# Normalised rows turned by VectorE and moved through DRAM: a one-core hybrid block

## The reference, cut to what matters

```
x = x + scan_layer(layernorm(x))      # projections, gated scan, product
x = x + ffn(layernorm(x))             # gelu(x @ W1t + b1) @ W2t + b2, hidden width 1024
x = x + attention(layernorm(x))       # 16 heads of 64, second-order linear attention
x = x + ffn(layernorm(x))             # the same weights again
```

## Time and profile before

| what | value |
|---|---|
| median of three executions | 1029.08 us (1025.98 to 1030.72) |
| the profiled execution, its own time | 1030.74 us |
| its span, first to last instruction | 1029.0 us |
| mean granted TensorE clock | 0.998 of full speed |
| TensorE busy | 1005.3 us |
| VectorE busy | 617.2 us |
| ScalarE busy | 491.0 us |
| first layer, to 97.3 us | TensorE busy 91.81 us |
| first feed-forward, 97.3 to about 227 us | tasks 16.06 us apart |
| attention, about 227 to 895 us | chunks some 20 us apart |
| last feed-forward alone, from 895.4 us | DMA share 0.11 |

### The profile page before, as it was taken

One profiled execution on the slowest core, in us unless ns is written; L12 is line 12 of the kernel. 1 busy time (PEld: TensorE's weight loads), 2 busy tenths in 40 slices (PEclk: granted clock), 3 DMA queues, 4 the chain that ended last, 5 costly groups with the idle time before them and its releaser, 6 DMA issues.

```text
span 1029.0 us, 41963 instructions
## 1 busy us (share of the span) xinstructions
PE 1005.3 (98%) x19166; PEld 909.2 (88%) x19166; DVE 617.2 (60%) x1252; ACT 491.0 (48%) x925; POOL 111.4 (11%) x130
## 2 busy tenths in 40 slices
PE   8999999999999999999999999999999999999998
PEld 7788798999998998899999999988899888889887
DVE  7888877763445545555465465553564457767773
ACT  5676766643343433333443344333443344456663
POOL 2461331220000000000000000000000000113130
PEclk9999999999999999999999999999999999999999
DMA  9422000023324233242242333332333333200101
GB/s 314 154 59 82 1 2 1 1 83 115 115 85 131 90 95 126 69 143 85 96 136 90 101 124 101 111 101 69 126 106 106 104 126 94 97 22 21 42 31 52
DMA packets 60735, 92.75 MB, mean 90 GB/s; under 512 B 7056, under 2 KB 50448, under 8 KB 59536
## 3 DMA queue, kind: packets, MB, share of 16 engines
q1 hardware_dynamic: 60288, 90.07, 26.6%
q10 hardware_dynamic: 272, 0.00, 0.0%
HBM read 48.63 MB, written 41.42 MB: 88 GB/s over the span
## 4 chain that ended last, share of the span: by engine, by line
PE 95%; ACT 2%; issue 1%; DVE 1%; POOL 0%; POOLq 0%; ACTq 0%; DVEq 0%
PE bank L223 7%; PE bank L224 6%; PE bank L1185 6%; PE bank L225 6%; PE bank L1211 6%; PE bank L1196 5%; PE bank L1245 4%; PE bank L1233 3%; PE bank L1175 3%; PE bank L1222 3%; PE bank L805 3%; PE bank L807 3%; PE bank L1246 3%; PE bank L1247 3%; PE bank L1261 3%; PE bank L1177 3%
## 5 line engine op out<-in xcount | busy, mean ns | idle before, releaser
L1471 ACT COPY qt<-bank 128x512 f32<-128x512 f32 x64 | 37.6, 587 | 157.0 <-PE bank L225 157.0
L1607 DVE STREAM_TRANSPOSE k<-kt 128x512 f32<-128x512 f32 x64 | 43.4, 697 | 106.6 <-ACT kt L1466 55.6
L1466 ACT COPY kt<-bank 128x512 f32<-128x512 f32 x64 | 37.5, 587 | 114.5 <-PE bank L225 114.5
L1628 DVE TENSOR_TENSOR state_s<-bank,state_s 128x256 f32<-128x256 f32 x124 | 46.8, 420 | 74.5 <-ACT ut L1484 72.5
L223 PE MATMUL bank<-ln_xhi,wk_hi 128*128 128x256 f32 x256 | 75.9, 296 | 0.0
L223 PE MATMUL bank<-ln_xhi,wq_hi 128*128 128x256 f32 x256 | 75.4, 294 | 0.0
L1245 PE MATMUL bank<-wo_hi,ot_hi 128*128 128x256 f32 x256 | 75.0, 293 | 0.0
L1518 ACT ACTIVATE D_hidden<-bank,b_sb 128x512 f32<-128x512 f32 x64 | 44.1, 690 | 59.6 <-PE bank L1262 59.6
L224 PE MATMUL bank<-ln_xlo,wk_hi 128*128 128x256 f32 x256 | 72.5, 283 | 0.0
L224 PE MATMUL bank<-ln_xlo,wq_hi 128*128 128x256 f32 x256 | 72.3, 283 | 0.0
L225 PE MATMUL bank<-ln_xhi,wk_lo 128*128 128x256 f32 x256 | 72.3, 282 | 0.0
(11 more groups left out here) (161 smaller groups left out, 2904.9 us busy)
## 6 DMA issues: line engine op xcount, KB each, us to landing
k_rows_scratch<-k SPq DMA_DIRECT2D x32, 512.0 KB, 2.7
k<-k_rows_scratch SPq DMA_DIRECT2D x128, 128.0 KB, 2.9
u_rows_scratch<-sc_and_k SPq DMA_DIRECT2D x31, 512.0 KB, 3.4
landed<-u_rows_scratch SPq DMA_DIRECT2D x124, 128.0 KB, 3.0
out_dram<-xres SPq DMA_DIRECT2D x16, 256.0 KB, 2.1
xres<-in_L_attn_a_x_dram SPq DMA_DIRECT2D x7, 512.0 KB, 10.5
w_nat<-in_L_ffn_W_dram SPq DMA_DIRECT2D x2, 1024.0 KB, 9.8
raw<-in_L_attn_b_W_q_dram SPq DMA_DIRECT2D x1, 1024.0 KB, 12.9
```

## The change

In both feed-forwards and in the attention the normalised rows are no longer turned by TensorE. VectorE turns 32x32 blocks of `ln.xn` into a tile (two instructions of 128x512), SyncE writes the tile to a DRAM scratch with one DMA, waits for it, and reads it back into `ln.xn` with four DMAs. ScalarE and VectorE then take `xhi` and `xlo` from SBUF instead of PSUM. The turns in the first layer stay with TensorE, and so does that of the first block of the first feed-forward. Where the rows go to the attention, the copies and subtractions are in quarters: four instructions of 128x256 instead of two of 128x512.

The order changes with it. In a feed-forward task the rows are normalised at f = 2 of the same task in which their statistics were taken at f = 1, and turned at f = 3, ahead of `xlo` at f = 4 (in task 1 of the last feed-forward they are normalised at f = 5 and turned at f = 6, and `xlo` moves from f = 6 to behind that). In the attention the statistics, the normalising and the turn come one chunk earlier (chunks 3 and 4 instead of 4 and 5, and so on), and `xhi` and `xlo` stay in chunk 5. The block of task (0,0) has its statistics in chunk 27 and is normalised and turned in chunk 28, that of (0,1) in chunks 28 and 29, and the next block of batch 0 is normalised and turned in chunk 31.

```diff
+            def dve_turn(self, dve, slot, tile, count):
+                if count:
+                    dve.wait_ge(self.rows_saved, 16 * count)
+                src = self.xn[:, slot, :, :].rearrange("p c d -> p (c d)").rearrange("p (n g f) -> p g n f", g=4, f=32)
+                for n in range(2):
+                    nc.vector.transpose(tile[:, :, 4 * n:4 * n + 4, :], src[:, :, 4 * n:4 * n + 4, :]).then_inc(self.rows_turned, 1)
+
+            def sp_move(self, sp, slot, tile, count):
+                if count:
+                    sp.wait_ge(self.rows_landed, 64 * count)
+                sp.wait_ge(self.rows_turned, 2 * (count + 1))
+                sp.dma_start(rows_dram["x"], tile.rearrange("p g n f -> p g (n f)")).then_inc(self.rows_saved, 16)
+                sp.wait_ge(self.rows_saved, 16 * (count + 1))
+                for g in range(4):
+                    sp.dma_start(self.xn[g * 32:(g + 1) * 32, slot, :, :],
+                                 rows_dram["x"].rearrange("(r p) g c -> g p r c", r=4)[g]).then_inc(self.rows_landed, 16)
...
+            def act_high_rows(self, act, b, count):
+                act.wait_ge(self.rows_landed, 64 * (count + 1))
                 for k in range(DC):
+                    nc.scalar.copy(self.xhi[:, b, k, :].rearrange("p (c r i) -> p c r i", c=CH, r=4),
+                                   self.landed(b, k)).then_inc(self.high_done[b], 1)
...
@@ first feed-forward, TensorE: the turns go @@
-                            if target and f == 3:
-                                prepare(target[0], target[2])
...
@@ first feed-forward, VectorE @@
-                        if target:
-                            tb, block_of_rows, n = target
-                            dve.wait_ge(ln.rstd_done[tb], START + n + 1)
-                            ln.dve_normalise(dve, tb, block_of_rows, n, ln_rstd)
...
+                            if f == 2:
+                                dve.wait_ge(ln.rstd_done[b], START + n0 + i + 2)
+                                ln.dve_normalise(dve, b, 0 if last else i + 1, n0 + i + 1, ln_rstd)
+                            if f == 3:
+                                dve.wait_ge(ln.normalised[b], START + (n0 + i + 2) * CH)
+                                ln.dve_turn(dve, b, turned, moves(b, i))
                             if target and f == 4:
-                                ln.dve_low(dve, tb, n, XB)
+                                ln.dve_low_rows(dve, target[0], target[2])
...
@@ attention, SyncE: the move goes behind keys and u; the last one ahead of the reload of W2 @@
+                    if norm_of(j):
+                        ln.sp_move(sp, norm_of(j) % 2, turned_x, chunk_moves(norm_of(j) - 2))
+                    if block_of(j) is not None:
+                        ln.sp_move(sp, block_of(j), turned_x, moves(block_of(j), 0))
...
+                ln.sp_move(sp, 0, k32, moves(0, 1))
                 sp.wait_ge(v_ready, 2 * CHUNKS)
                 sp.dma_start(wv_hi[:, :, :].rearrange("p a b -> p (a b)").bitcast(FP32), w2t_dram).then_inc(w2_loaded, 16)
...
@@ attention, VectorE @@
+                    elif block_of(j + 1) is not None:
+                        if block_of(j + 1) == 0:
                             dve.wait_ge(x_added, 8)
+                        ln.dve_statistics(dve, block_of(j + 1), 0, nd)
                     if norm_of(j):
+                        chunk_normalise(norm_of(j) - 2)
+                    elif block_of(j) is not None:
+                        normalise_for(block_of(j), 0)
+                        turn_for(block_of(j), 0, turned_x)
...
@@ ScalarE: the first gelu of the last feed-forward (its tile shares memory with the turned rows) @@
+                    if n == 0:
+                        act.wait_ge(ln.rows_saved, 16 * (moves(1, 0) + 1))
...
@@ last feed-forward, VectorE @@
+                        if f == started + 2 and i + 1 < NBLK:
+                            normalise_for(b, i + 1)
+                        if f == started + 3 and i + 1 < NBLK:
+                            turn_for(b, i + 1, k32)
+                        if target and f == high_at(t):
+                            ln.dve_low_rows(dve, target[0], nd + target[1])
```

More of the change, by code:

```diff
@@ L753, in sync @@
                 sp.dma_start(w2t_dram, w2t.rearrange("p a b -> p (a b)").bitcast(FP32)).then_inc(w_saved, 16)
+                for i in range(NBLK):
+                    for b in range(B):
+                        ln.sp_move(sp, b, turned, moves(b, i))
                 sp.wait_ge(out_ready[0], START + 2 * NBLK)
@@ L810, in down @@
                         last.then_inc(out_ready[b], 1)
[L812 to L817, removed]
                 def iteration(i, first, last):
                     for b in range(B):
[L821 removed]
+                        behind = former(b, i, first)
                         for f in range(FC):
@@ L833, in tail @@
                 def tail():
[L834 to L837, removed]
+                    for part in range(FC):
+                        down(1, NBLK - 1, part)
                 steps(iteration, tail)
@@ L868, in tail @@
                     for b in range(B):
+                        act.wait_ge(ln.rows_landed, 64 * (moves(b, NBLK - 1) + 1))
                         for k in range(DC):
[L870 to L873, removed]
+                            for s in range(2):
+                                last = nc.scalar.copy(of_turns(ln.xhi, s, k, b), landed_of_turns(b, k, s))
+                            last.then_inc(ln.high_done[b], 1)
                 steps(iteration, tail)
@@ L924, in tail @@
                             dve.wait_ge(ln.high_done[b], START + (n0 + NBLK) * DC + k + 1)
[L925 to L928, removed]
+                            for s in range(2):
+                                last = nc.vector.tensor_tensor(of_turns(ln.xlo, s, k, b), landed_of_turns(b, k, s),
+                                                               of_turns(ln.xhi, s, k, b).bitcast(FP32), ALU.subtract)
+                            last.then_inc(ln.low_done[b], 1)
                         add_rows(1, NBLK - 1, b)
@@ L1686, in chunk_low, with turn_for @@
                         dve.wait_ge(x_high, 2 * m + k + 1)
-                        nc.vector.tensor_tensor(chunked(ln.xlo)[:, slot, k, :, :, :].rearrange("p q b t -> p b q t"),
-                                                bank[XB[k]][:, :].rearrange("p (b q t) -> p b q t", b=B, q=4),
-                                                chunked(ln.xhi)[:, slot, k, :, :, :].rearrange("p q b t -> p b q t").bitcast(FP32),
-                                                ALU.subtract).then_inc(x_low, 1)
+                        for b in range(B):
+                            last = nc.vector.tensor_tensor(of_turns(ln.xlo, slot, k, b), landed_of_turns(m, k, b),
+                                                           of_turns(ln.xhi, slot, k, b).bitcast(FP32), ALU.subtract)
+                        last.then_inc(x_low, 1)
+                def turn_for(b, i, tile):
+                    dve.wait_ge(ln.normalised[b], START + (nd + i + 1) * CH)
+                    ln.dve_turn(dve, b, tile, moves(b, i))
                 dve.wait_ge(before.w_saved, 32)
```

163 lines of the change are left out of this document (70 added, 93 removed).

## The result

The changed kernel takes 1038.5 us (median of 9 runs, 1031.6 to 1039.7) where the kernel before takes 1027.9 beside it: ratio 1.0086, interval 1.0066 to 1.0106. It is slower by more than 0.5%, and 1.5 us above the top of the range. The profiled execution is 8.0 us longer in its span (1037.0 against 1029.0), where the sum had nothing. Of the executions of the kernel before that ran beside the experiments, two (1377 and 5457 us, the others 1025 to 1032) are in no ratio.

A forecast was written before the change was run, and what follows sets the result against it. The prediction took TensorE to bound the kernel (busy 1005.3 of 1029.0 us); 19.1 us saved against 19.1 us of losses gave a median of 1029 us. Range: 1017 to 1037 for 8 in 10, likeliest case 1024 to 1034.

The forecast's parts named there:

- the sum: Whole kernel: 19.1 us saved against 19.1 lost, 1030.7 us for the profiled execution; chance 0.45 for 1024 to 1034.
- The saving: Transposes taken off TensorE: 0.88 us for each of 16 feed-forward groups, 0.83 for six in the attention; 19.1 us, upper bound.
- Item 1: First task of the first feed-forward: VectorE waits for rstd, then stands under the bias; loss 3.8 us.
- Items 2 and 5: Five tasks after the first feed-forward's first, and last feed-forward's tasks 2 to 4: 0.65 us stall each, 3.3 and 2.0.
- Item 3: Last task of the first feed-forward: `low` 7, handed to the tail, comes late for its first part down; loss 1.8 us.
- Item 4: Last feed-forward, task 1: `xlo` comes 1.0 us later and TensorE is there 0.88 earlier; loss 1.9 us.
- Item 6: Last feed-forward, task 5: two biases fall on the normalising, a third on `low` 4, delaying `xlo`; loss 4.4 us.
- Attention: Six chunks save 0.83 us each; chunks 28 and 29 lose 1.3 and 0.45, from 30 on 1.35 returns, net loss 0.4.
- W2: End of attention: the reload of W2, behind the last move, is issued at 899.4 and lands late; loss 1.5 us (0.5 to 3).
- The first: Rival: VectorE's normalising does not stand under GpSimd's bias; losses 5.0, time 1015 us; chance 0.28 with partial cases, whole 0.1.
- rows that landed late: Rival: the rows' DRAM round trip exceeds 9.8 us and stalls ScalarE at `xhi`; at 11 us in nine tasks 1040; chance 0.05.
- VectorE slower than counted: Rival: extra VectorE work ahead of `xlo` counts in 14 places; at 0.5 us a task 1036 us; chance 0.22.

The follow-up runs named there:

- the fillers: Changed kernel with products that nothing reads put on TensorE ahead of four of its waits: 1033.7 us, ratio 1.0043 against the kernel before.
- all five edits: Changed kernel with bias behind next normalising, last two biases later, first-task statistics earlier, W2 reload before last move, task 2's `xlo` before normalising: 1015.1 us, ratio 0.9872.

## Why the prediction was wrong, point by point

**The saving**: right. 19.1 counted, 18.6 by doing the transposes twice, and 0.88 a task where nothing is in the way (15.18).

**Item 1, first task**: right. The first part down is at 115.26 instead of 111.1, 4.2 late where 3.4 stands; with the fillers it is at 114.69, so 0.6 of the 4.2 is the clock. VectorE waits for rstd and then stands under the bias, as said; timelines of VectorE and GpSimd in the changed kernel:

```profile
106.74 3.41 DVE L171 TENSOR_SCALAR ln_xn<-xres,ln_moments,ln_rstd 128x256 f32<-128x256 f32 x4 [1.18 <-POOL ln_rstd L164]
110.06 0.68 DVE L928 TENSOR_TENSOR B_hid_lo<-B_hidden,B_hid_hi 128x512 fp32r<-128x512 f32 x1
110.67 1.29 DVE L182 STREAM_TRANSPOSE B_turned<-ln_xn 128x512 f32<-128x512 f32 x2
```

```profile
106.67 2.36 POOL L813 TENSOR_TENSOR xres<-xres,b_sb 128x1024 f32<-128x1024 f32 x1
```

**Items 2 and 5, steady tasks**: right. 15.80 us from rstd to rstd in both feed-forwards (15.8 foretold), 0.62 above the 15.18 without a wait where 0.65 stands. The rows of TensorE show 1.7 of waiting in five tasks of the first one, some 0.34 each, and the rest is in the steps around them. Timeline of GpSimd in the changed kernel:

```profile
136.26 0.56 POOL L161 TENSOR_TENSOR ln_vare<-ln_moments,ln_eps 128x4 f32<-128x4 f32 x1 [13.17 <-DVE ln_moments L156]
...
137.89 2.41 POOL L813 TENSOR_TENSOR xres<-xres,b_sb 128x1024 f32<-128x1024 f32 x1
152.06 0.56 POOL L161 TENSOR_TENSOR ln_vare<-ln_moments,ln_eps 128x4 f32<-128x4 f32 x1 [11.76 <-DVE ln_moments L156]
```

**Item 3, tail**: right, a wait of 1.5 for `low` (1.8).

**Item 4, task 1**: right. TensorE waits 3.3 for `xlo` where it waited 1.5: 1.8 more (1.9).

**Item 6, task 5**: right in kind; 3.1 where 4.4 stands (a wait of 3.5, less the 0.4 of the other tasks). Two biases fall on the normalising and the third on `low`, as said:

```profile
982.76 5.56 DVE L171 TENSOR_SCALAR ln_xn<-xres,ln_moments,ln_rstd 128x256 f32<-128x256 f32 x4 [1.19 <-POOL ln_rstd L164]
```

```profile
982.70 4.82 POOL L1202 TENSOR_TENSOR xres<-xres,b_sb 128x1024 f32<-128x1024 f32 x2
988.40 2.75 POOL L1202 TENSOR_TENSOR xres<-xres,b_sb 128x1024 f32<-128x1024 f32 x1 [0.88 <-DVE ln_xn L171]
```

**Attention**: right in the six chunks, open in the whole. The chunks that had transposes take as long as those without (20.07), as chunk 5 in the changed kernel's timeline of VectorE, where the earlier trace rows have 20.90:

```profile
340.86 1.29 DVE L1649 TENSOR_TENSOR state_z<-bank,state_z 128x512 f32<-128x512 f32 x2 [1.83 <-PE bank L1291]
...
360.93 1.29 DVE L1649 TENSOR_TENSOR state_z<-bank,state_z 128x512 f32<-128x512 f32 x2 [0.58 <-PE bank L1291]
```

TensorE waits 1.1 for `sc_b` in chunk 28 and 0.5 in 29 (1.3 and 0.45), 0.3 in 30. From the first to the last addition the nine traces that have this attention take 611.8 to 618.3 us, mean 615.6, against 621.3 in the one of before: -5.7 where -6.4 stands. The profiled execution itself gained only 3.6. The spread is in pauses of TensorE that end with no wait ("issue"), 7.1 to 10.9 us of them in these traces and 8.3 in the one of before, and in the clock behind them: six of the nine have a fall there and take 616.5 on average, the three without take 613.7.

The -5.7 flatters the change. The traced execution of the kernel before is 2.8 us above that kernel's median, the nine are 0.6 below their own medians on average. If these distances lie in the attention, which is an assumption, the gain there is 2.3 (an estimate), 4.1 less than the sum has. Together with the 4.4 of the clock that would be nearly the whole miss. I have not tested what sets the pauses, so this half stays open.

**W2**: mis-sized, inside its bounds. Issued at 900.56 (899.4), 6.0 from issue to landing (5.5 taken), a wait of 2.4 in the profiled execution and 2.8 to 3.0 in five others, where 1.5 stands. The landing times that the prediction gives, 904.1 to 907, make 0.7 to 3.6 and not its "0.5 to 3".

**The step that failed** is none of the items but the way they were added: "losses 3.8 + 3.3 + ... = 19.1" prices each wait at its length. Two kinds of loss differ. The short waits of the steady tasks cost what the sum has (0.62 each), with the clock at 1.00 throughout. A wait of 2 to 4 us can also bring the granted clock down to its lower level behind it. The sum had four such waits (items 1, 4, 6 and W2) and no term for it, and no chance for it among the rivals either; by the run with the fillers that term is 4.4 us, half of the miss. Stage by stage the miss of the profiled execution is 2.4 + 2.8 + 2.8. The 2.4 of the first feed-forward is the clock (1.8, and 0.6 to 1.8 against other traces) and small differences of the items. The 2.8 of the attention is the half that stays open (above). The 2.8 of the last one is the clock (3.3) and W2 (0.9), less item 6 (-1.3).

**The rivals.** The first, priced at 1015, measured 1021.4 as an experiment: 6 us too low, with no term for the clock and too little for the W2 wait. No wait of TensorE in the steady tasks goes back to rows that landed late. "VectorE slower than counted" did not occur: its pieces came out as counted. The changed kernel landed where that rival stands, for another reason; that the measured time is near its 1036 is chance.

## What to carry to other kernels

When a sum of gains and losses on a bound TensorE comes out even, look at what the losses are made of: take the clock from the windows behind every wait or pause of some microseconds, in the kernel before as well, for a gain that is spread thin does not pay for a few long waits. When the sum is carried from one traced execution to a median, ask first how far that execution is from its own median (here 2.8 us). Before a two-input operation is moved from PSUM to SBUF, look at what GpSimd runs beside it, and hold that back by a later count of a semaphore that exists already. Here the same change made the time 0.9% longer or 1.3% shorter, by where five groups of instructions stand in their queues.

## What the runs showed of the hardware

The fall of the clock is not fixed by the length of the wait. Behind waits of 1.9, 2.4, 3.0, 3.5 and 3.9 us it came, and behind pauses of 2.0 in the attention of both kernels; behind one wait of 1.7 it did not. The wait of 3.3 at task 2 has 1.00 behind it in the changed kernel and 0.66 in the run with W2 ahead; the wait of 2.9 for W2 has 1.00 in the run with `xlo` earlier, and 0.50 in the runs with the statistics earlier and with the bias nearly left out. The Trainium skill calls the clock's phase run-variable at the start of a kernel (TensorE: Matmul & The Clock Gate, What's actually happening); these rows show the like in its middle. It goes with the spread of the changed kernel's executions, 8.1 us over nine, where the shortest has the highest mean clock; those with all five edits lie 2.3 apart (four). That the clock makes the spread is not shown.

Beside a GpSimd addition that reads SBUF, a VectorE subtraction with two SBUF inputs is held up (5.62 instead of 1.28) and so is normalising (5.56 and 3.41 instead of 1.38), while a 32x32 transpose from SBUF to SBUF is not (1.29). That a two-input subtraction waits for the whole GpSimd instruction agrees with the lock that the Trainium skill describes (SBUF — State Buffer, SBUF: two separate sides).
